# All attention products in TensorE tiles of 64 rows by 32 columns, with two score slots and outputs in two banks

## What is computed

```python
xn = layernorm(x)                                   # no scale, no bias
x1 = layernorm(xn[:, :, :128] + mha(xn[:, :, :128], ...1), g1, be1)
xs = holt(xn)                                       # level and trend, one step per token
x2 = layernorm(xs[:, :, :128] + mha(xs[:, :, :128], ...2), g2, be2)
y = concatenate([x1, x2])
a = layernorm(y + relu(y @ w_ff1.T + b_ff1) @ w_ff2.T + b_ff2, g_ff, be_ff)
f = relu(xn @ W1 + b1) @ W2 + b2                    # 256 -> 1024 -> 256
out = x + a + f
```

## Time and profile before

| | us |
|---|---|
| median of three runs | 2529.78 |
| the profiled execution, its own time | 2531.42 |
| its span | 2529.9 |
| TensorE matmul busy | 2454.3 (97%) |
| ScalarE busy | 2183.1 (86%) |
| VectorE busy | 1355.8 (54%) |
| GpSimd busy | 366.7 (14%) |
| granted TensorE clock, mean | 0.993 |

### The profile page before, as it was taken

One profiled execution on the slowest core, in us unless ns is written; L12 is line 12 of the kernel. 1 busy time (PEld: TensorE's weight loads), 2 busy tenths in 40 slices (PEclk: granted clock), 3 DMA queues, 4 the chain that ended last, 5 costly groups with the idle time before them and its releaser, 6 DMA issues.

```text
span 2529.9 us, 66513 instructions
## 1 busy us (share of the span) xinstructions
PE 2454.3 (97%) x29057; PEld 961.8 (38%) x29057; DVE 1355.8 (54%) x3059; ACT 2183.1 (86%) x2419; POOL 366.7 (14%) x315
## 2 busy tenths in 40 slices
PE   6899999999999999999999999999999999999996
PEld 4233333336633333334653333333564333333354
DVE  5344445557744444455783444444577444445576
ACT  5899999986499999997569999999656999999953
POOL 1100110003500020000450002000063001100053
PEclk9999999999999999999999999999999999999998
DMA  8200120006110030000611004000151001200001
GB/s 223 78 10 10 36 40 14 6 6 129 51 60 10 10 61 10 10 6 6 141 48 50 10 10 61 10 10 6 46 105 51 10 10 25 47 10 10 6 30 43
DMA packets 49675, 95.95 MB, mean 38 GB/s; under 512 B 7888, under 2 KB 32464, under 8 KB 48992
## 3 DMA queue, kind: packets, MB, share of 16 engines
q1 hardware_dynamic: 42880, 76.92, 11.1%
q0 software_dynamic: 6496, 14.69, 4.0%
HBM read 57.45 MB, written 34.08 MB: 36 GB/s over the span
## 4 chain that ended last, share of the span: by engine, by line
PE 87%; DVE 7%; ACT 3%; issue 1%; POOL 1%; DMA 1%; SPq 0%; DVEq 0%; ACTq 0%; POOLq 0%
PE slot L1484 34%; PE slot L1458 19%; PE slot L1244 16%; PE slot L1517 6%; PE slot L1533 5%; DVE rden L873 2%; PE slot L1362 2%; ACT p_sb L738 2%; DVE hid_one L905 1%; PE slot L1371 1%; DVE rden L866 1%; POOL p_sb L612 1%; DVE den L868 1%; PE slot L1309 1%; PE slot L1347 1%
## 5 line engine op out<-in xcount | busy, mean ns | idle before, releaser
L738 ACT ACTIVATE p_sb<-slot 128x1024 f32<-128x1024 f32 x2048 | 1904.6, 1031 | 74.5 <-PE slot L1458 74.5
L1484 PE MATMUL slot<-p_sb,v_sb 128*17 128x512 f32 x8192 | 1069.3, 596 | 8.2 <-ACT p_sb L738 8.1
L1458 PE MATMUL slot<-q_st,k_st 50*128 50x512 f16 x4096 | 621.9, 382 | 6.4 <-ACT p_sb L738 3.2
L1458 PEld LDWEIGHTS slot<-q_st,k_st 50*128 50x128 f16 x4096 | 117.1, 94 | 876.0 <-ACT p_sb L738 871.5
L917 DVE SCALAR_TENSOR_TENSOR second<-slot,second 128x256 f32<-128x256 f32 x64 | 27.2, 424 | 593.3 <-PE slot L1244 593.3
L1484 PEld LDWEIGHTS slot<-p_sb,v_sb 128*17 128x17 f32 x8192 | 181.4, 96 | 226.9 <-ACT p_sb L738 207.5
L905 DVE TENSOR_SCALAR hid_one<-slot,b_grown 128x256 f32<-128x256 f32 x256 | 123.7, 483 | 241.3 <-PE slot L1244 238.5
L1244 PE MATMUL slot<-xt_parts,w_parts 128*32 128x256 f16 x6144 | 214.8, 274 | 9.0 <-DVE hid_one L905 9.0
L1244 PE MATMUL slot<-w_parts,hid_parts 128*32 128x256 f16 x6144 | 214.7, 274 | 0.0
L1244 PEld LDWEIGHTS slot<-xt_parts,w_parts 128*32 128x32 f16 x6144 | 140.8, 96 | 121.4 <-issue 95.4
L1244 PEld LDWEIGHTS slot<-w_parts,hid_parts 128*32 128x32 f16 x6144 | 140.6, 96 | 110.7 <-issue 108.6
(11 more groups left out here) (117 smaller groups left out, 1733.7 us busy)
## 6 DMA issues: line engine op xcount, KB each, us to landing
part_dram<-p_sb SPq DMA_DIRECT2D x16, 1024.0 KB, 4.1
xn<-x SPq DMA_DIRECT2D x16, 512.0 KB, 6.2
second<-x SPq DMA_DIRECT2D x32, 256.0 KB, 3.2
ffn_dram<-second SPq DMA_DIRECT2D x32, 256.0 KB, 2.0
area<-ffn_dram SPq DMA_DIRECT2D x16, 512.0 KB, 5.1
out<-area SPq DMA_DIRECT2D x15, 512.0 KB, 3.2
k_st<-part_dram SPq DMA_DIRECT2D x24, 256.0 KB, 11.6
k_st<-part_dram POOLq DMA_DIRECT2D x48, 128.0 KB, 4.9
```

The source lines that it names most:

```text
L738: act.activation(p_sb[:, n % 4, :], slot[n % 3][:, :], ACT.Exp, scale=0.25 / GROW ** 2).then_inc(exp_done, 1)
L1458: mm = pe.matmul(slot[at % 3][:, k * CHUNK:(k + 1) * CHUNK], k_st[rows_, pair, kt * P:(kt + 1) * P], q_st[rows_, pair, c_ * CHUNK:(c_ + 1) ...
L1484: mm = pe.matmul(o_bank[ROW * j:ROW * j + DK + 1, :], v_sb[:, a, kt, GH * g + j, :], p_sb[:, n % 4, (j % 2) * CHUNK:(j % 2 + 1) * CHUNK], ...
```

## The change

- Scores, values, the second network and the projection use tiles of 64 rows by 32 columns, eight side by side. Scores: each half is 8 matmuls where it was 2. Values, network and projection: each product is split in two by its contraction rows, 0 to 63 and 64 to 127, and twice as many matmuls are issued.
- The two halves of such a product go to two banks (`o_banks` in `slot[2]`, `sides` in `slot[3]`), so that each result is the sum of two banks. VectorE adds them: the eviction becomes two copies (after which the bank is free), an add and a shuffle; a hidden tile becomes four operations where it was three, the bank free after the second; an output tile and the projection each get one operation more.
- Scores go round two slots where they went round three, and are issued as: first half of the next step, what is planned, second half, values.
- VectorE's work on a pair of units is put later among the hidden tiles, the projection goes from step 7 to 11 and waits for six hidden tiles where it waited for four, and the hidden tiles' steps move.
- The prologue's third smoothing and the last batch's first transposes, which write `slot[2]`, wait for the eviction.

```diff
-HIDDEN_KTS, OUT_KTS, PROJECTION_KT = [0, 2, 3, 5, 9, 11, 12, 14], [0, 2, 4, 6, 8, 10, 12, 14], 7
+HIDDEN_KTS, OUT_KTS, PROJECTION_KT, BEFORE_PROJECTION = [0, 2, 4, 6, 8, 10, 13, 14], [0, 2, 4, 6, 8, 10, 12, 14], 11, 6
...
-            o_bank, side = slot[3][:, 0:CHUNK], slot[3][:, CHUNK:]
+            o_banks, sides = [slot[2][:, r * CHUNK:(r + 1) * CHUNK] for r in range(2)], [slot[3][:, r * CHUNK:(r + 1) * CHUNK] for r in range(2)]
...
-                        act.activation(p_sb[:, n % 4, :], slot[n % 3][:, :], ACT.Exp, scale=0.25 / GROW ** 2).then_inc(exp_done, 1)
+                        act.activation(p_sb[:, n % 4, :], slot[n % 2][:, :], ACT.Exp, scale=0.25 / GROW ** 2).then_inc(exp_done, 1)
...
                     hold(dve, pv_done, TILES * (u + 1) + 2)
-                    dve.stream_shuffle(o_sb[:, n % 2, :], o_bank, O_ROWS[n % 2]).then_inc(o_read, 1)
+                    step(dve.tensor_copy(rden[:, :], o_banks[0]))
+                    dve.tensor_copy(o_sb[:, n % 2, :], o_banks[1]).then_inc(o_read, 1)
                     hold(dve, o_read, u + 2)
+                    step.settle()
+                    step(dve.tensor_tensor(rden[:, :], rden[:, :], o_sb[:, n % 2, :], ALU.add))
+                    step.settle()
+                    step(dve.stream_shuffle(o_sb[:, n % 2, :], rden[:, :], O_ROWS[n % 2]))
+                    step.settle()
...
-                    dve.tensor_tensor(part, side.rearrange("p (t n) -> p t n", t=CT), part, ALU.add).then_inc(out_read, 1)
+                    step(dve.tensor_tensor(part, sides[0].rearrange("p (t n) -> p t n", t=CT), part, ALU.add))
+                    step.settle()
+                    dve.tensor_tensor(part, sides[1].rearrange("p (t n) -> p t n", t=CT), part, ALU.add).then_inc(out_read, 1)
...
-                    dve.tensor_scalar(hid_one[:, :], bank, b1_grown[:, k:k + 1], 0.0, ALU.add, ALU.max).then_inc(hid2_read, 1)
+                    step(dve.tensor_scalar(hid_one[:, :], sides[0][:, cols], b1_grown[:, k:k + 1], None, ALU.add))
+                    step.settle()
+                    dve.tensor_tensor(hid_one[:, :], sides[1][:, cols], hid_one[:, :], ALU.add).then_inc(hid2_read, 1)
                     dve.wait_ge(hid2_read, n + 1)
-                    step(dve.tensor_copy(hid_hi[:, k, :], hid_one[:, :]))
-                    step.settle()
-                    dve.tensor_tensor(hid_lo[:, k, :], hid_one[:, :], hid_hi[:, k, :], ALU.subtract).then_inc(hid2_ready, 1)
+                    step(dve.tensor_scalar(hid_hi[:, k, :], hid_one[:, :], 0.0, None, ALU.max))
+                    step.settle()
+                    dve.scalar_tensor_tensor(hid_lo[:, k, :], hid_one[:, :], 0.0, hid_hi[:, k, :], ALU.max, ALU.subtract).then_inc(hid2_ready, 1)
...
-                                invert(0)
                             hidden_half(b, i, 1)
                             if n > 0:
-                                invert(1)
+                                invert(0)
                             hidden_half(b, i, 2)
                             if n > 0:
-                                attended(b, n - 1)
+                                invert(1)
                             hidden_half(b, i, 3)
                             if n > 0:
-                                add_projection(b, n - 1)
+                                attended(b, n - 1)
                             hidden_half(b, i, 4)
                             if n > 0:
                                 check_sums(b, n - 1)
-                            for k in range(5, HB):
+                            hidden_half(b, i, 5)
+                            if n > 0:
+                                add_projection(b, n - 1)
+                            for k in range(6, HB):
                                 hidden_half(b, i, k)
...
-                def narrow(out, lhs, rhs, start, stop):
-
-                    for r in range(P // ROW):
-                        mm = pe.matmul(out[ROW * r:ROW * (r + 1), :], lhs[:, ROW * r:ROW * (r + 1)], rhs, start=start, stop=stop,
-                                       skip_group_check=True)
+                def side_product(cols, lhs, rhs, start, stop):
+
+                    for j in range(P // ROW):
+                        for r in range(2):
+                            rows_ = slice(HALF * r, HALF * (r + 1))
+                            mm = pe.matmul(sides[r][ROW * j:ROW * (j + 1), cols], lhs[rows_, ROW * j:ROW * (j + 1)], rhs[rows_, :],
+                                           start=start, stop=stop, skip_group_check=True)
...
-                        pe.wait_ge(hid2_read, HB * (HALVES * b + i) + 4)
+                        pe.wait_ge(hid2_read, HB * (HALVES * b + i) + BEFORE_PROJECTION)
...
+                        if k == 2 and before is not None:
+                            pe.wait_ge(o_read, UNITS2 * b + 1)
...
+                        pe.wait_ge(exp_done, UNITS2 * STEPS * b + at - 1 + 3)
+                        pair = GH // 2 * g + n
+                        for r in range(P // ROW):
+                            for k in range(2):
+                                rows_ = slice(HALF * k, HALF * k + ROWS)
+                                mm = pe.matmul(slot[n][ROW * r:ROW * (r + 1), k * CHUNK:(k + 1) * CHUNK],
+                                               k_st[rows_, pair, kt * P + ROW * r:kt * P + ROW * (r + 1)],
+                                               q_st[rows_, pair, c_ * CHUNK:(c_ + 1) * CHUNK], start=True, stop=True, skip_group_check=True)
...
+                        for j in range(GH):
+                            n = 2 * kt + j // 2
+                            for r in range(2):
+                                rows_ = slice(HALF * r, HALF * (r + 1))
+                                mm = pe.matmul(o_banks[r][ROW * j:ROW * j + DK + 1, :], v_sb[rows_, a, kt, GH * g + j, :],
+                                               p_sb[rows_, n % 4, (j % 2) * CHUNK:(j % 2 + 1) * CHUNK],
+                                               start=(kt == 0), stop=(kt == TILES - 1), skip_group_check=True)
...
+                            if more:
+                                scores(at)
                             if kt in net_kts:
                                 (second_out_part if unit % 2 else second_hidden)(b, unit // 2, net_kts.index(kt))
                             if kt == PROJECTION_KT and unit > 0 and unit % 2 == 0:
                                 out_projection(b, unit - 1)
...
+                            if more:
+                                scores(at + 1)
+                            values(unit, kt)
...
                     attention(b)
+                    pe.wait_ge(o_read, UNITS2 * (b + 1) + 1)
```

## The result

The changed kernel takes 2664.36 us (median of four runs, 2658.14 to 2668.82) against 2529.78 for the kernel before measured beside it: a ratio of 1.0527, 95% interval 1.0509 to 1.0545. The direction was forecast and the time lies inside the range, but the loss is 134.6 us where 47 were forecast. The profiled execution took 2658.1 us.

The account below looks back on a forecast made before the run. TensorE sets the pace, ScalarE's floor close below; after the change ScalarE and its waits bind. Odd units +13, even +28, first -4, outside 8.5: +46 on 2531.4, so 2577 us; range 2515 to 2680.

Parts of the forecast that it names:

- The new tiles: Attention steps: one tile shape removes the 0.10 us gaps; two steps cost TensorE 3.3 us, so ScalarE's 3.66 becomes the bound.
- Two slots at nothing: Scores in two slots: slack of about 0.1 us, so no cost given; 0.1 us a unit, 6 in all, inside the range.
- The eviction: Unit boundaries: two copies out of PSUM before the next values lose 0.7 us at each of a batch's 15 boundaries.
- VectorE's chain: Even units: VectorE reads the sixth hidden tile at 23.95 us, so TensorE waits 1.85 before the projection; unit 31.9 against 30.88.
- The first unit: First unit of each batch: no such VectorE chain, eight steps at 1.83 and eight at 1.98 us; 30.5 against 31.42.
- a rival on issue: Attention matmuls: TensorE's issue becomes the bound at 28 ns a pair of weight load and matmul; 2800 us, chance 23%.
- Its milder form: Attention matmuls: half the issue rival's effect, about 2650 us; half of that rival's 23% chance.
- Outside the attention: Batch ends: VectorE's queue moves by 2.1 us, 2.3 more three times, 1.6 after the last batch; 8.5 us together.
- The cover of 0.33: Between attentions: the first state's copy ended 0.33 us ahead of TensorE's need, so 1.7 us comes on the path.
- a chain that fits: Even units: the sixth read comes by 22.1 us, so the 28 waits go; 2527 us, no change, chance 9%.
- copies that hide: Chain fits and the two copies are over 0.35 us earlier: units 29.7 on both sides; 2504 us, chance 9%.

Follow-up runs that it names:

- The kernel that has only the pieces: Kernel before, old tiles, slots and bank kept, each attention matmul cut along its moving columns into as many pieces as the change makes; 2595.2 us, ratio 1.0260.
- all four repairs: Changed kernel with check of the sums later, next x loaded in unit 2, second branch's loads one a tile step, states copied before the reciprocals; 2572.8 us, ratio 1.0165.

## Why the prediction was right and wrong

**The new tiles: right.** "If twice as many matmuls stream side by side in the same time" held to the hundredth: parts of 48 in 0.65, values 0.87, the gaps of 0.10 gone, and with them TensorE's hold on the bound. By the Trainium skill, "TensorE: Matmul & The Clock Gate", section on 56 ns against 53.3, starts never come closer than about 25 ns; 0.65 us for 48 matmuls is 13.6 ns each, so for side-by-side tiles the trace contradicts it, as the sum had assumed.

**Two slots at nothing: right.** Odd units have no hole but the boundary's; without the second copy they are 29.44, ScalarE's own pace.

**The eviction: right.** 0.7 us a boundary forecast; ScalarE's idle time 0.58 and the overlap of 0.11 that each restart loses make 0.69. Odd units 30.0 as forecast, and 29.44 without the copy.

**VectorE's chain: right, a little small.** Sixth read forecast at 23.95 and found at 24.17; wait of 1.85 forecast, ScalarE idle 2.00 and 0.11 of restart. Behind the projection come 0.2 more of slips, so 32.3 for 31.9. Moving the check away returned the unit to 30.5.

**The first unit: the step that failed.** The forecast was 30.5, better than before, "8 with TensorE's 0.44 + 0.87 + 0.67": it took TensorE as free to run through the densest steps of the program. It came out at 33.8 to 37.8. The prediction did hold a rival on issue, but with the wrong form. It looked for a price of each pair of instructions, to be paid in every part; at 13.6 ns a matmul no such price shows. (Its milder form gave about 2650, near the time measured, and the range reached 2680 through it and the chain: that the time lies inside is luck.) What is bounded is the supply: the doubled instructions come as 494 packets of 16 KB over the same 16 DMA engines that carry the data. Beside a burst of loads the packets come late and TensorE stands mid-part. The row that would have told of it, the instruction queue's 230 packets, was on the page before, and the prediction read nothing from it. The size: 17 us more in the first units where 4 less were forecast, 21; the eighth and ninth units 30 (against 30.0 and 32.3 each); 4 in the other even units (779.6 against 24 x 32.3). That is 55 us, put down to supply by where it lies; the 16 stops alone are 38 of it, 14.8 in the first units, and the rest was not taken apart. The kernel that has only the pieces shows 48 more in its first, eighth and ninth units. Three things tie the holes to the packets: more packets in old tiles bring them, loads taken out or spread remove them where they were, and each stop ends just behind a packet. No run moved the packets themselves. The first unit of the last batch, with no x to load, is still at 33.8: other data (1.03 MB from 2045 to 2049) fills the DMA engines up to 2048.5, TensorE stops at 2050.11 for 1.45 us, ScalarE stands idle 1.88 there, and the steps behind it come as the packets do. Where no stop falls a dense step took 1.97 us (2057.35 to 2059.32), so the streaming in the forecast's 1.98 was right.

**Outside the attention: right in kind, a third of its size.** The cover of 0.33 was gone and TensorE waited 1.87 us where 1.7 were put. But the wait was priced at its own length, the second step that failed. The granted clock fell after it in two of three places, and the smoothing that follows ran at half speed, 2.07 us for a block of 1.12. At the full clock the stretch was 136.2, 2.7 more than before, near the 2.3 forecast; at the low one 141.9 and 143.4. With the wait gone all three were 135.0.

**The sum.** From the forecast's 2577 to the profiled 2658.1: supply 55, clock and the rest outside 24 - 8.5 = 15, the chain 28 x 0.4 = 11, that is 81. Two terms that the sum did not hold, supply and clock, are some seven eighths of the miss of this execution.

**The rivals on the fast side** (a chain that fits, copies that hide) did not come: both waits were there, at their size. The best version found, all four repairs, takes 2572.8 us and is still 1.65% slower than the kernel before. What is left in its profile: 11 us in the 32 odd units, the second copy; 10 in the first units; 8 in the other even ones; 6 between the attentions and 6 at start and end.

## What to carry to other kernels

Where a change multiplies instructions, read the instruction queue's packets and ask where the stream is densest and where the DMA engines are full; a burst of loads that cost nothing before may then stop TensorE, and pacing it is a cheap repair (22 us of the 30 here). A wait on TensorE in a thin stretch should be priced with the clock that follows: 1.6 us of wait cost up to 9.6. And to take TensorE off the bound is worth only what the next engine leaves, here 0.3 us of an odd unit, while every added read of a second PSUM bank goes on VectorE's chain at once.

## What the runs showed of the hardware

- TensorE ran 48 matmuls of 64 rows by 32 columns, 256 columns wide, in 0.65 us, 13.6 ns from one to the next, with their weight loads beside them.
- About 0.10 us stood at each change between the scores' and the values' tile shape in the kernel before (0.96 from values to scores, whose streaming is 0.87), and none where all had one shape.
- 256 TensorE instructions come in one packet of 16 KB, over the 16 DMA engines. In the changed kernel no two packets started less than 3.28 us apart. With the engines full, TensorE stood up to 4.0 us in the midst of a group of matmuls; with little other traffic, 0.96 to 1.37 us.
- After a wait of 1.64 us the granted clock went to 0.50 within the next few us and stood there over the 8 us shown, in a kernel that runs at 1.00 there without it.
- Each restart of ScalarE's row of exponentials costs 0.11 us beyond the idle time, the overlap of one with the next (1.03 us long, 0.917 apart).
